# Graph attention with residual and norm: the last columns of five blocks are written by SP, row by row, in place of five of POOL's scatters

## What is computed

```python
proj = einsum('ni,rio->nro', x, relation_weight)
att = sum(proj[src, etype] * tanh(proj[dst, etype] + efeat), axis=-1)
a = exp(att - seg_max[dst]) / seg_sum[dst]              # softmax over the edges of one dst
h_nb = segment_sum(x[src] * a, dst)
r = leaky_relu((x + h_nb) @ res_fc_w.T) + leaky_relu(x * h_nb @ res_fc2_w.T)
out = layernorm(x + r)
```

## Time and profile before

| | |
|---|---|
| time, median of 3 runs | 746.59 us (746.47 to 746.75) |
| the profiled execution: its time, and its span | 746.59 us, 744.7 us |
| busy: PE, DVE, ACT, POOL | 75%, 80%, 66%, 75% of the span |
| granted TensorE clock, mean | 0.914 |
| indirect DMAs on POOL | 388 gathers, 196 scatters, 2 for the ends |
| row DMAs on SP | 512, in 32 chunks |
| DMA traffic | 70.37 MB, 94 GB/s |

### The profile page before, as it was taken

How to read it: one execution, slowest core, us unless ns; L and a number is a source line. 1 busy time by engine, 2 the same in 40 slices (tenths; PEclk the granted TensorE clock), 3 DMA queues, 4 the chain that set the end, 5 groups by cost and what they waited for, 6 DMA issues and landing times. The chain is left out here.

```text
span 744.7 us, 14060 instructions
## 1 busy us (share of the span) xinstructions
PE 561.5 (75%) x4172; PEld 344.6 (46%) x4172; DVE 594.9 (80%) x1094; ACT 491.0 (66%) x1401; POOL 560.5 (75%) x594
## 2 busy tenths in 40 slices
PE   3888989989988988998998889898888896300000
PEld 2454556556555655655655545444444455200000
DVE  3789999999999999999999999999999986400010
ACT  1287778779878978987987897556655567600040
POOL 6777777777777777777777777777777777777776
PEclk9999999999999999999999999999999998555555
DMA  4554354354344434434533333311222110000000
GB/s 112 166 172 130 86 153 127 87 153 132 98 151 141 139 85 154 127 90 150 147 98 104 113 112 109 81 57 58 75 77 69 47 35 32 25 18 18 19 18 17
DMA packets 48033, 70.37 MB, mean 94 GB/s; under 512 B 15970, under 2 KB 19486, under 8 KB 47958
## 3 DMA queue, kind: packets, MB, share of 16 engines
q1 hardware_dynamic: 18562, 32.97, 14.7%
q0 software_dynamic: 18752, 17.29, 11.0%
q10 hardware_dynamic: 10644, 19.23, 6.9%
HBM read 45.60 MB, written 25.78 MB: 96 GB/s over the span
## 5 line engine op out<-in xcount | busy, mean ns | idle before, releaser
L440 POOL DMA_INDIRECT xsd<-in_x,ends_i x388 | 366.7, 945 | 119.1 <-issue 108.0
L957 DVE SCALAR_TENSOR_TENSOR xm<-typ,xT_ps 128x1024 f32<-128x1024 f32 (+1 forms) x225 | 264.0, 1183 | 0.3 <-ACT xc L691 0.3
L464 POOL DMA_INDIRECT out<-out_r,row_i x196 | 190.7, 973 | 59.7 <-issue 56.0
L548 PE MATMUL t_ps<-xm,w_rel 64*64 64x512 f32 (+1 forms) x900 | 223.3, 603 | 5.3 <-DVE xm L957 3.8
L550 PE MATMUL h_ps<-xm,w_rel 64*64 64x512 f32 (+1 forms) x900 | 223.3, 603 | 0.0
L567 PE MATMUL y_ps<-bd_cat,dT 128*128 128x256 f32 x392 | 99.7, 399 | 26.6 <-DVE zd L1030 22.9
L548 PEld LDWEIGHTS t_ps<-xm,w_rel 64*64 64x64 f32 x900 | 55.8, 134 | 98.8 <-issue 49.5
L715 ACT ACTIVATE o_t<-zd,rstd 128x64 f32<-128x64 f32 x392 | 98.5, 334 | 0.8 <-ACT o_t L715 0.5
L567 PEld LDWEIGHTS y_ps<-bd_cat,dT 128*128 128x128 f32 x392 | 72.4, 195 | 51.2 <-issue 22.4
L998 DVE SCALAR_TENSOR_TENSOR es<-es,wd,wx 128x64 f32<-128x64 f32 x196 | 55.3, 282 | 17.5 <-issue 14.3
L575 PE MATMUL tr_ps<-ident,uw 128*128 128x128 f32 x196 | 33.8, 298 | 34.2 <-DVE uw L1053 33.3
(11 more groups left out here) (152 smaller groups left out, 880.4 us busy)
## 6 DMA issues: line engine op xcount, KB each, us to landing
x_in<-in_x SPq DMA_DIRECT2D x48, 256.0 KB
typ<-typ_d SPq DMA_DIRECT2D x24, 512.0 KB
out<-o_t ACTq DMA_DIRECT2D x48, 256.0 KB
xsd<-in_x SPq DMA_DIRECT2D x512, 0.2 KB
xsd<-in_x,ends_i POOLq DMA_INDIRECT x388
hist<-es ACTq DMA_DIRECT2D x24, 256.0 KB, 2.0
ea<-in_edge_attr SPq DMA_DIRECT2D x24, 224.0 KB
out<-out_r,row_i POOLq DMA_INDIRECT x196, 2.1
```

The source lines that it names most:

```text
L440: pool.indirect_dma_start(xsd[:, s % RX, j, side, :], None, x[:, :], bass.IndirectOffsetOnAxis(ap=ends_i[:, side, c:c + 1], axis=0),).then ...
L464: pool.indirect_dma_start(out[:, :], bass.IndirectOffsetOnAxis(ap=row_i[:, c:c + 1], axis=0), out_r[:, s % RW, j, :], None, bounds_check=t ...
L548: pe.matmul(t_ps[h * D:(h + 1) * D, 0:n], w[0:D, :], moving[0:D, h * n:(h + 1) * n], start=(at == 0), stop=(at == R - 1), skip_group_check ...
L957: v.scalar_tensor_tensor(xm[:, m % RM, 0:n], typ[:, s % RT, 0:n], float(r), xT_ps[:, 0:n], ALU.is_equal, ALU.mult).then_inc(masked, 1)
```

## The change

POOL's `scatter` leaves out the last column of blocks 8, 9, 10, 11 and 12. SP writes these rows itself, 16 rows to a chunk, with a range check on the register that holds the address: a row whose index lies over the bound is skipped as a whole. For this DVE makes the byte offsets of the five columns (`out_at`, in `rows()`, pass 2), SP stores them to DRAM with rows and columns exchanged (pass 4) and loads them back (pass 5), so that a chunk's 16 offsets lie side by side. There are 40 chunks: two in each of the passes 18 to 24, behind the loads of the pass, and 26 behind the last pass. SP's gathers, 32 chunks as before, now come two in every pass, so that they end with pass 16.

```diff
     for s in range(1, NS):
-        n = (2 if s % 2 else 1) if s * 3 < ND else 2 if s % 2 else 1
+        n = 2
         CHUNKS[s], left = left[:n], left[n:]
...
+    OUT_BLOCKS, OUT_STEPS = [8, 9, 10, 11, 12], range(18, NS)
+    def out_columns(s):
+        return [j for j in range(cols(s)) if not (s in OUT_BLOCKS and j == cols(s) - 1)]
+
+    OUT_CHUNKS = [[] for s in range(LAST + 2)]
+    left = list(range(len(OUT_BLOCKS) * PARTS))
+    for s in OUT_STEPS:
+        OUT_CHUNKS[s], left = left[:2], left[2:]
+    OUT_CHUNKS[LAST + 1] = left
...
+            def save_out_at():
+                sp.wait_ge(out_at_done, len(OUT_BLOCKS))
+                sp.dma_start(rows_d.rearrange("k p -> p k"), out_at[:, :], allow_slow_non_contiguous=True).then_inc(out_at_saved, DMA)
+
+            def load_out_ids():
+                sp.wait_ge(out_at_saved, DMA)
+                sp.dma_start(out_ids[:, :], rows_d[:, :]).then_inc(out_ids_in, DMA)
+
+            def rows_to(n):
+                k, part = divmod(n, PARTS)
+                s, p0 = OUT_BLOCKS[k], part * CHUNK
+                j = cols(s) - 1
+                if n == 0:
+                    sp.wait_ge(out_ids_in, DMA)
+                    for m in range(RO):
+                        sp.wait_ge(o_stored[m], o_need(m))
+                if part == 0:
+                    sp.wait_ge(fmul_done, s + 1)
+                ids = [sp.alloc_register(f"to{n}_{i}") for i in range(CHUNK)]
+                sp.load(ids, out_ids[k:k + 1, p0:p0 + CHUNK])
+                for i in range(CHUNK):
+                    at = sp.snap(ids[i], donate=True, min_val=0, max_val=(N - 1) * ROW)
+                    sp.dma_start(out_bytes[bass.DynSlice(at, ROW)].rearrange("(a c) -> a c", a=1),
+                                 out_r[p0 + i:p0 + i + 1, s % RW, j, :].bitcast(U8), bounds_check="skip_entire_dma").then_inc(rows_out[k], DMA)
...
                 for n in mine[2:]:
                     rows_at(n)
+                if s == 4:
+                    save_out_at()
+                if s == 5:
+                    load_out_ids()
+                for n in OUT_CHUNKS[s] if s > 0 else []:
+                    rows_to(n)
+
+            for n in OUT_CHUNKS[LAST + 1]:
+                rows_to(n)
+            for k in range(len(OUT_BLOCKS)):
+                sp.wait_ge(rows_out[k], P * DMA)
...
-                for j in range(cols(s)):
+                for j in out_columns(s):
...
+                for k, s in enumerate(OUT_BLOCKS):
+                    c = s * COLS + cols(s) - 1
+                    v.tensor_scalar(out_at[:, k:k + 1], row_i[:, c:c + 1], float(4 * D), None, ALU.mult).then_inc(out_at_done, 1)
```

More of the change, by code:

```diff
@@ L98, in columns @@
         return [(j, side) for side in range(2) for j in range(cols(s)) if not (s in ROW_BLOCKS and (j, side) == (cols(s) - 1, 1))]
+    def out_columns(s):
[5 more added lines that the diff above has]
+    OUT_CHUNKS[LAST + 1] = left
+    assert min(OUT_BLOCKS) >= NS - RW and all(cols(s) == COLS for s in OUT_BLOCKS)
     E_NEED, e_count = [], [0] * RE
@@ L106, in gnn_resnorm @@
     typ_d = nc.dram_tensor("typ_d", [T, P], F32).ap()
+    rows_d = nc.dram_tensor("rows_d", [len(OUT_BLOCKS), P], I32).ap()
     with ExitStack() as ctx:
@@ L150, in gnn_resnorm @@
         row_ids = sb("row_ids", [len(ROW_BLOCKS), P], I32)
+        out_at = sb("out_at", [P, len(OUT_BLOCKS)], I32)
+        out_ids = sb("out_ids", [len(OUT_BLOCKS), P], I32)
         xsd = sb("xsd", [P, RX, COLS, 2, D])
@@ L211, in gnn_resnorm @@
         scattered = sems("scattered", RW)
+        out_at_done, out_at_saved, out_ids_in = sem("out_at_done"), sem("out_at_saved"), sem("out_ids_in")
+        rows_out = sems("rows_out", len(OUT_BLOCKS))
         xT_done, masked, quad_done, eadd_done = sem("xT_done"), sem("masked"), sem("quad_done"), sem("eadd_done")
@@ L383, in rows_at @@
                                  x_bytes[bass.DynSlice(at, ROW)].rearrange("(a c) -> a c", a=1)).then_inc(rows_in[k], DMA)
+            out_bytes = out.rearrange("n f -> (n f)").bitcast(U8)
+            def save_out_at():
[20 more added lines that the diff above has]
+                                 out_r[p0 + i:p0 + i + 1, s % RW, j, :].bitcast(U8), bounds_check="skip_entire_dma").then_inc(rows_out[k], DMA)
             load_e(0)
@@ L484, in _ @@
             for k in range(RW):
-                pool.wait_ge(scattered[k], sum(cols(s) for s in range(k, NS, RW)) * DMA)
+                pool.wait_ge(scattered[k], sum(len(out_columns(s)) for s in range(k, NS, RW)) * DMA)
             pool.wait_ge(fix_out, DMA)
```

## The result

Over four runs each the ratio is 1.0237 (95% interval 1.0221 to 1.0253). The profiled execution took 764.64 us with a span of 762.9, so it stands for the median.

A forecast was written before the change was run, and what follows sets the result against it. POOL, bound by its DMA count, gives way to SP: 581.7 + 194.1 for 30 chunks = 775.8; (b) +14.4 and (c) -14.5 cancel; + 3.45 + 1.92 = 781 us, 4.6% slower. Range 750 to 815, chance 0.85.

The forecast's parts named there:

- POOL's part: Five column scatters leave POOL: 6.4 us less, its last issue ending at 734.8 instead of 741.22.
- Where the tail starts: SP's 30 chunks in a row behind the last typ load start at 580.97 + 0.7 for DVE's five new instructions.
- The register load and the written row: SP's cost per chunk: 1.257 us to load 16 ids, 0.32 us per row with gaps, 6.47 us a chunk.
- (a): A row written to DRAM from SP costs between 7% less on the DMA (-7.7 us) and equal; equal was taken.
- (b): The range check on SP's row writes: ends 0 and +58 us; 0.03 us a row taken, +14.4 us.
- (c): 121 of the tail's 480 rows are skipped by the check: 0 to 31.5 us less; 0.12 each taken, -14.5 us.
- The end: From the last issue to the end of the span: 3.45 us, as behind POOL's last issue before.
- The transposed store: SP's store of 640 elements of 4 bytes in pass 4: some 4.7 us of SP, hidden.
- Pass 13: SP waits 26 us for z2_done of block 11; loads behind it issue at about 395 to 403; hidden, 0 us.
- The sign in "what would show it": If the forecast is right, the profile's chain that ended last is SP's and not POOL's.
- The ring behind SP: Rival: SP's small writes drain slower than SP issues, each landing before the next, about 1445 us; chance 0.03.

The follow-up runs named there:

- five_blocks: The change with three chunks a pass from pass 17 on, 22 instead of 30 behind the last typ load; 740.05 us, ratio 0.9914.
- the kernel of four: The change with blocks 8 to 11 only, 22 chunks in SP's tail, on chips where before takes about 898 us; 961.92 us, again 959.05 us.
- change_here: The change itself, unaltered, timed again where the kernel before took 746.73 us; 763.35 us, ratio 1.0228.
- experiments 9 to 12: Four runs where before takes about 747 us: three_blocks 742.81 us, change_here 763.35, all_unchecked 782.85, five_blocks 740.05.
- all_unchecked: The change without range check, all 640 rows written to different rows of a scratch tensor, the five columns not written to the output; 782.85 us.
- gather_order: The kernel before with only SP's gathers moved to two chunks in every pass, on a slow chip; 898.36 us, ratio 1.0002.
- the control: The kernel before, unchanged, run once more on a slow chip; 896.93 us.
- three_blocks: The change with blocks 8, 9 and 10 only, three chunks a pass from pass 17, six behind the last typ load; 742.81 us, ratio 0.9947.

## Why the prediction was right, and what was mis-sized

The call (slower, SP the bound by 30 chunks in one piece behind the last typ load, POOL some 5 us earlier and idle at the end) was right, and 764.7 lies in the range. The size was not: a loss of 34 us was forecast, 18 were measured, and the centre, 781, was 16.3 us too high. That it still lies in the range is owed to the range's width. By its own terms:

- **POOL's part** was right: 6.4 us less was given, and five_blocks collects it. In the profiled execution of the change its DMAs were 2 to 3 ns slower (948 and 975 against 945 and 973), which is 1.7 us on 579 of them; in five_blocks they were not (945 and 972), and line 535 issues 6.5 us earlier than line 481. Executions differ by this without any change: the kernel of four has 949 on one slow chip and 945 on the other.
- **Where the tail starts**: 583.3 against 581.7. DVE's five instructions (+0.7) are not to be seen: in change_here the typ load of pass 1 stands 0.46 us late against before and the last one 0.49. The 2.3 us of the first trace arose in the first 42 us, where change_here, the same kernel, had 0.5; so they are not a cost of the five instructions. But the other three traces of experiments 9 to 12 have 2.2 to 2.3 there too, and what makes it isn't shown.
- **The register load and the written row** were right: 1.229 us for 16 ids on the median of 40, 0.320 from one written row's DMA to the next. Here writes issue like reads, so (a) at "equal" held.
- **(b), the range check**, is the term that was mis-sized most. It was put at 0.03 us a row, +14.4 us, from POOL's 0.973 against 0.945. That pair differed in direction too, and the check on SP costs nothing (0.227 us with and without).
- **(c), the skipped row**, went the right way and was a little small: 0.12 us less was taken, 0.149 is in the changed kernel's timeline (0.171 between starts in place of 0.320), 18.0 us for 121 rows and not 14.5. A skip is neither free nor as dear as a write; that the middle of two far ends came near was partly luck. The prediction let (b) and (c) cancel; measured, one is 0 and the other -18.
- (b) and (c) together explain 18 us. Some 2 come back as small pauses: a tail in which every row is written took 196.6 us (all_unchecked), where the prediction's 30 chunks make 194.1; from one written row to the next it is 0.331 us on the mean, not 0.320. 178.3 us were measured for the tail, 194.0 predicted with (b) and (c).
- **The end**: 1.3 us lie between SP's last issue and the end of the span, not the 3.45 that followed POOL's: 2.15 less. The sum 781.1 + 1.6 - 15.8 - 2.15 - 0.2 (time over span 1.74, not 1.92) is 764.6.
- **The transposed store** was put at 4.7 us of SP by the strided load's 0.93 us for 127 elements. It took 0.427 for 640. Hidden either way, but a wrong analogy: of these two DMAs the one with five times the elements took half the time.
- **Pass 13**: predicted SP idle for 26 us and loads at 395 to 403, no cost. Seen: 26.2 us, loads about 2 us behind those times, as everything in this execution, no cost; gather_order confirms it.
- **The sign in "what would show it"** that failed: the chain that ended last didn't become SP's. The page builds it from busy work, and it counts none for SP.
- **The ring behind SP** did not fall back. 457 rows were written, and the last landed within 0.8 us. In the trace each written row is one packet of 256 bytes and one of 4, and a skipped row is none: from 740 us on 61 row DMAs were issued, 12 of them skipped, and 98 packets moved.
```profile
q1 hardware_dynamic: 98, 0.01, 0.4%
...
out<-out_r SPq DMA_DIRECT2D x61, 0.2 KB
```
- **The register load once more.** With the 200 ns a register that the Trainium skill states (Runtime: NRT & Kernel Launch, Instruction fetch mechanics) the estimate for 16 ids is 3.2 us. The trace has 1.23 and decides.

What stays open: on the slow chips, why SP and POOL paused between instructions, and why a chunk of the tail took 10 to 11 us on the mean until POOL had ended. TensorE's granted clock was lower there as well (0.91 in the control from 100 to 600 us, 0.99 before from 100 to 500); whether that is a cause isn't shown. The change itself wasn't run there; the 22 chunks that fit elsewhere made both kernels 7% slower. So the margin of five_blocks, 20.9 us of SP's idle, doesn't carry to every chip. three_blocks, with six chunks in the tail, would by an estimate fit there too: the first six chunks of the tail of four took 53 us, and SP's idle end in the control is 135. That wasn't tried.

## What to carry to other kernels

A queue that shows 160 us of waiting at the end is not 160 us of free room for everything moved to it: lay out which instructions fall behind its last scheduled work, multiply by the interval from start to start in its own timeline (6 us a chunk here), and compare with the time at which the bound engine will end. With eight more chunks in the passes in which the queue waits anyway, the same DMAs gained 6.8 us; with these eight behind the passes they lost 18. Look at the end of the span in the timeline of every queue, because a chain built on busy time can't name one that only issues.

## What the hardware showed that was not expected

In these traces a single-row DMA from SP with its address in a register starts every 0.32 us, read or write. If its range check drops it, it holds SP for 0.073 us, the next starts after 0.171, and no packet moves; the check itself adds nothing to one that passes (0.227 us with and without). The store of 640 elements of 4 bytes held SP for 0.427 us, less than the 0.93 of a strided load of 127. Two chips ran the kernel before at 898 us in place of 747, with unchanged durations of POOL's DMAs; there pauses of some 0.7 us stand between some of SP's row DMAs, where the changed kernel's trace has mostly 0.03 to 0.04.
